# A transformer block on one core: mLSTM cells as two chunks of 128 positions with a carried state, two heads per exponential, product and score bank

## The chip, the cores and the metric

The kernel runs on one core of a Trainium2 chip, as one launch. The metric is the device time in microseconds (us) of that launch, less is better. The engines named below are TensorE (PE; PEld is its weight load), VectorE (DVE), ScalarE (ACT), GpSimd (POOL) and SyncE (SP), which issues most transfers.

## The reference

Four sublayers act on x of 4 x 256 tokens with 256 features: a cross attention, a mixture of 8 expert FFNs (one shared, seven routed), an mLSTM cell, and an FFN with 4-bit block quantisation. The change is in the third one. With queries q from the layer norm of x, keys and values both from `ctx`, 16 heads of 16 features, 256 positions s and t:

```
log_f = log_sigmoid(fg);  log_f_cum = cumsum(log_f)
log_D[s, t] = log_f_cum[s] - log_f_cum[t] + ig[t]   (t <= s, else -inf)
max_log_D = max over t;  D = exp(log_D - max_log_D)
C = (q k^T / sqrt(16)) * D
h = C / (max(|sum_t C|, exp(-max_log_D)) + eps) @ v
h = layer norm over each head's 16 features, times ln_scale
```

## The kernel before

Tokens are worked on in two halves of two batches. The order of all steps is one hand-written list, `step_order` (line 121): each engine walks through the same list and performs its part of the steps that it has. `weave(main, side)` (line 102) spreads the side list over the main one in proportion to TensorE items. Engines are in order, and wait for each other by semaphores.

The cells of half 0 are spread over the experts of half 1 (`expert(k)`, line 159: `gate` and `up` twice, `out` twice, weight splitting, and one step of FFN weight quantisation, `mx_quantise` and `mx_grids`). The cells of half 1 run near the start of the FFN (`stage_d`, line 223), with little beside them.

For each half, `prepare` (line 207) makes the gates: `gate_rows` (a matmul, 32 rows for each batch), `gate_math` on DVE (line 1517: a running sum, a running maximum, and the maximum split into three bf16 parts that six copies place in `mb`), and `q_split`, which cuts the queries into bf16 parts that go through DRAM and come back stacked. `turn_gates` (line 922) waits on TensorE for the end of `gate_math` and for an exponential on ACT, and turns the gate rows into columns `geT`.

Then come 32 cell units w for each half (64 in all), one per head and batch. A unit has the keys as rows, the queries as columns, and only the causal part: 256 columns for keys 0 to 127 and 128 columns for keys 128 to 255.
- `cell_exponent` (lines 933 and 1166): three bf16 matmuls of 256, 256 and 128 columns place the causal mask and minus the running maximum in a bank; ACT takes the exponential in two instructions, each with the key's own gate as a bias column.
- `cell_score` (lines 947 and 1543): two bf16 matmuls of 256 and 128 columns give the scores; DVE multiplies both into `probs` (384 columns).

`cell_bank` (line 87) gives the half 0 units one bank for exponents (4) and one for scores (5); in half 1 there are three of each. So in half 0 the scores of unit w + 1 wait until DVE has done the product of unit w.

Eight units make a group g. `cell_values` (line 959) multiplies them with the values, with f32 matmuls of 32 output rows, four side by side in the array; `cell_values_copy`, `turn3` and `cell_normalise` (line 1554) finish the group. `finish` (line 211) does the head norm and the next layer norm.

## Time and profile before

| | |
|---|---|
| median of 3 runs | 485.39 us |
| the three runs | 485.39, 479.90, 485.39 us |
| the profiled execution | 480.16 us |
| its span, first to last instruction | 478.3 us |
| mean granted TensorE clock | 0.921 of full |
| busy | PE 77%, DVE 75%, ACT 39%, POOL 33% |

The span is what the trace covers; 1.9 us of the profiled execution lie around it. The profiled execution is at the lower of the two levels that the runs show, 5.2 us under the median. Times below count from the span's start.

### The profile page before, as it was taken

Reading aid. Unit: us, or ns where it says so; the run is one execution under the profiler, and the core shown is the slowest. Engines: PE = TensorE matmul, PEld = TensorE weight load, DVE = VectorE, ACT = ScalarE, POOL = GpSimd, SP = SyncE. Lnnn points to the kernel's source line nnn. Section 1 sums busy time; section 2 is a strip of 40 time slices with the busy share of each in tenths; the row PEclk is TensorE's granted clock in tenths of the full one; section 3 lists DMA queues with packets and bytes.
Section 4 is the critical chain, followed back from the end, with each engine's and each line's share of the span. In section 5 each row is a group of like instructions: output and inputs, shape, how many; then the busy total and the mean of one; then the engine's idle time right before and its main releaser. Section 6 shows DMA issues by size and latency. Waiting matters only on the chain.

```text
span 478.3 us, 6936 instructions
## 1 busy us (share of the span) xinstructions
PE 367.9 (77%) x2330; PEld 248.8 (52%) x2330; DVE 359.5 (75%) x857; ACT 188.4 (39%) x331; POOL 155.6 (33%) x147
## 2 busy tenths in 40 slices
PE   7899788999999678957948888977656488650764
PEld 4576456545568457846635565656533156430333
DVE  4588348685549999699796667569995986789895
ACT  4456427233232204412354354533005488540331
POOL 4019400087416325554325413123412110031240
PEclk9999999899999879999979999999888789976687
DMA  8900000032120222234973911824000760000001
GB/s 281 254 28 1 10 1 2 0 112 84 48 67 14 75 89 88 89 88 115 227 123 82 172 56 46 131 57 56 0 1 0 122 122 1 2 0 6 18 19 47
DMA packets 33713, 32.67 MB, mean 68 GB/s; under 512 B 3876, under 2 KB 32784, under 8 KB 33680
## 3 DMA queue, kind: packets, MB, share of 16 engines
q1 hardware_dynamic: 31088, 28.99, 26.1%
q0 software_dynamic: 992, 1.68, 1.1%
q10 hardware_dynamic: 1600, 1.57, 1.0%
q8 instruction: 19, 0.31, 0.3%
q14 instruction: 14, 0.11, 0.1%
HBM read 28.04 MB, written 4.19 MB: 67 GB/s over the span
## 4 chain that ended last, share of the span: by engine, by line
PE 45%; DVE 31%; issue 12%; ACT 8%; POOL 3%; DVEq 0%; ACTq 0%; POOLq 0%
PE bank L870 10%; PE bank L782 5%; PE bank L896 5%; PE bank L755 3%; PE bank L798 3%; PE bank L1006 2%; PE bank L970 2%; DVE mxraw L1624 2%; DVE x L1458 2%; DVE mam L1466 2%; DVE probs L1551 2%; PE bank L766 2%; PE bank L918 2%; PE bank L832 1%; ACT probs L1078 1%
## 5 line engine op out<-in xcount | busy, mean ns | idle before, releaser
L870 PE MATMUL bank<-tok_r,probs_r 128*128 128x512 f32 x104 | 46.6, 448 | 17.4 <-DVE wT L1447 9.7
L896 PE MATMUL bank<-wexp,wT 128*128 128x256 f32 x192 | 53.5, 403 | 6.0 <-DVE x L1458 5.9
L1128 ACT ACTIVATE silu_sb<-bank 128x512 f32<-128x512 f32 x32 | 19.1, 598 | 79.3 <-PE bank L870 79.3
L673 POOL TENSOR_TENSOR wexp_r<-wexp,probs_r 128x1024 fp32r<-128x1024 f32 x13 | 31.3, 2409 | 48.1 <-ACT probs_r L1089 48.1
L1325 DVE TENSOR_SCALAR probs<-probs,hi 128x512 f32<-128x512 f32 x64 | 35.0, 599 | 14.8 <-ACT probs L1078 14.7
L591 POOL TENSOR_TENSOR mx_grid<-parts,bl 128x1024 bf16<-128x1024 fp8e4 x9 | 17.2, 1908 | 88.5 <-DVE parts L1627 88.5
L1078 ACT ACTIVATE probs<-bank 128x1024 f32<-128x1024 f32 x32 | 32.2, 1026 | 29.8 <-PE bank L782 29.8
L896 PEld LDWEIGHTS bank<-wexp,wT 128*128 128x128 f32 x192 | 36.6, 200 | 13.1 <-issue 6.7
L1551 DVE SCALAR_TENSOR_TENSOR probs<-bank,dexp 128x384 f32<-128x384 f32 x48 | 26.5, 555 | 21.2 <-PE bank L956 15.3
L870 PE MATMUL bank<-tok_r,wexp_r 128*128 128x512 f32 x104 | 41.7, 401 | 0.0
L576 POOL TENSOR_TENSOR mxraw<-mxraw,mx_grid 128x512 f32<-128x512 f32 x12 | 15.3, 1278 | 69.6 <-DVE mx_grid L1492 69.6
L782 PE MATMUL bank<-qrep,krep 32*128 32x256 f32 x256 | 33.8, 393 | 2.2 <-ACT probs L1078 1.2
L1175 ACT ACTIVATE dexp<-bank,geT 128x256 f32<-128x256 f32 x48 | 23.2, 483 | 27.9 <-PE bank L944 27.8
L870 PEld LDWEIGHTS bank<-tok_r,probs_r 128*128 128x128 f32 x104 | 20.2, 194 | 24.2 <-DVE wT L1447 11.0
L782 PEld LDWEIGHTS bank<-qrep,krep 32*128 32x128 f32 x256 | 23.1, 184 | 13.7 <-issue 12.3
L955 PE MATMUL bank<-qrep,krep 128*128 128x256 bf16 x64 | 18.0, 281 | 15.5 <-DVE probs L1551 13.6
L996 PE MATMUL bank<-identb,mx_grid 128*128 128x128 bf16 x80 | 8.7, 274 | 27.1 <-POOL mx_grid L591 19.9
L1006 PE MATMUL bank<-ctx,wexp 128*128 128x512 bf16 x64 | 23.0, 519 | 8.0 <-DVE wexp L1636 5.8
L1458 DVE SCALAR_TENSOR_TENSOR x<-bank,cw,x 128x256 f32<-128x256 f32 x64 | 27.5, 475 | 0.1
L1447 DVE SCALAR_TENSOR_TENSOR wT<-silu_sb,bank 128x512 f32<-128x512 f32 x24 | 16.4, 685 | 12.8 <-PE bank L870 5.8
L870 PE MATMUL bank<-xnT_r,probs_r 128*128 128x512 f32 x64 | 25.6, 400 | 0.0
L870 PE MATMUL bank<-xnT,wexp 128*128 128x512 f32 x48 | 24.7, 642 | 0.0
(261 smaller groups left out, 891.1 us busy)
## 6 DMA issues: line engine op xcount, KB each, us to landing
wexp<-in_L_ffn_W SPq DMA_DIRECT2D x28, 256.0 KB, 4.0
krep<-part_dram SPq DMA_DIRECT2D x32, 128.0 KB, 5.3
qrep<-part_dram SPq DMA_DIRECT2D x32, 128.0 KB, 4.8
wexp<-in_L_ffn_Wg SPq DMA_DIRECT2D x14, 256.0 KB, 4.3
part_dram<-parts POOLq DMA_DIRECT2D x4, 384.0 KB, 3.0
part_dram<-parts SPq DMA_DIRECT2D x4, 384.0 KB, 2.6
x<-in_x ACTq DMA_DIRECT2D x2, 512.0 KB, 7.2
ctx<-in_ctx SPq DMA_DIRECT2D x2, 512.0 KB, 6.9
```

Of the source, the lines that this page charges most:

```text
L673: gp.tensor_tensor(low, raw, w_high[k % 2].bitcast(F32), ALU.subtract).then_inc(s["w_low_ready"], 1)
L782: m = pe.matmul(bank[:, bk + q, S * kc:S * kc + S], krows[strip, jj % 2, c, S * b + P * kc:S * b + P * kc + P], qrows[strip, c, S * b:S * ...
L870: mm = pe.matmul(bank[:, bk, :], lhs, rhs, start=(kk == 0 and q == 0), stop=(kk == KC - 1 and q == len(terms) - 1))
L896: mm = pe.matmul(bank[:, 2 + pair, D * t:D * t + D], hid[k % 2][m][:, col:col + P], wexp[:, k % WR, 2, m, :], start=(m == 0), stop=(m == 1))
L955: pe.matmul(bank[:, bk, 0:S], krep[:, slot, j, col:col + P], qrep[:, slot, j, col:col + S], start=True, stop=True)
L1006: m = pe.matmul(bank[:, 2 * (y % 2) + r, :], xqT[:, k, P * i:P * i + P], wt[:, k, 512 * hf:512 * hf + 512], start=(k == 0), stop=(k == KC ...
L1078: act.activation(score_probs(u), bank[:, bk:bk + 2, :], ACT.Exp, scale=1.0 / float(np.sqrt(HD))).then_inc(s["exp_done"], 1)
L1128: act.activation(silu_sb[:, w % 2, :], bank[:, 0, :], ACT.Silu if direct else ACT.Tanh, scale=1.0 if direct else 0.5).then_inc(s["sigmoid_ ...
L1175: act.activation(dexp_slot(w)[:, 0:S], bank[:, bk, 0:S], ACT.Exp, bias=geT[:, n, 0, 0, row:row + 1]).then_inc(s["d_done"], 1)
L1325: ins = v.tensor_scalar(w, w, hi[:, 2 * b + kc:2 * b + kc + 1], EM50, ALU.min, ALU.max)
L1458: v.scalar_tensor_tensor(x[:, i, :], bank[:, 2 + pair, D * t:D * t + D], cw[:, i, e:e + 1], x[:, i, :], ALU.mult, ALU.add).then_inc(s["x2_ ...
L1551: v.scalar_tensor_tensor(probs[:, g % 2, j, 0:384], bank[:, cell_bank(w)[1], 0:384], 1.0 / float(np.sqrt(HD)), dexp_slot(w), ALU.mult, ALU ...
```

## The change

A batch's 256 positions are cut into two chunks of 128. Inside a chunk the cell is computed as before, with a mask, exponents, scores and values of 128 x 128. What the queries of chunk 1 get from the keys of chunk 0 no longer goes through exponents and scores. The keys of chunk 0, weighted by their decay up to position 127, are multiplied with the values into a state of 16 x 17 for each head (`state`), the queries of chunk 1 are weighted by their own decay (`spread`, `qstate`), and two f32 matmuls of 128 x 128 x 128 for each group add state times query into the values' bank.

A unit is now two heads. Its exponents are four blocks of 128 columns that fill a bank (512 columns), its scores four matmuls of 128 columns, with one exponential and one product for both. There are 16 units for each half, four to a group. The key's gate is no bias column of the exponential any more but is added in the matmuls, from a second row that `mb` now carries, so the split into bf16 parts and the six copies are 512 wide.

`gate_math` is cut into `gate_scan`, `gate_split`, `gate_decay` and `gate_place`. `turn_gates` moves from ahead of the cells to behind the first unit, and the cells of half 0 begin behind expert 10's last step instead of within that expert. POOL's share of the quantisation moves from the list's `mx_quantise` to its `mx_grids`, and POOL builds a few more constants.

```
 def cell_bank(w):
-    return (4, 5) if w < 32 else (w % 3, 3 + w % 3)
+    return (4, 5) if w < 16 else (w % 3, 3 + w % 3)
...
-        for j in range(8):
-            w = 8 * g + j
+        for j in range(4):
+            w = 4 * g + j
...
             if g > first:
-                if j == 2:
+                if j == 1:
                     u = st("cell_values", g - 1) + u + st("cell_values_copy", g - 1)
-                if j == 5:
+                if j == 3:
                     u = st("turn3", g - 1) + u + st("cell_normalise", g - 1)
+            if g % 4 == 0:
+                u = [[], st("turn_gates", g // 4), st("spread", g // 4), st("state", g // 2)][j] + u
+            if g % 4 == 1 and j == 2:
+                u = st("state", g // 2 + 1) + u
...
-            + st("gate_rows", n) + st("q_split", 2 * n) + st("gate_math", n) + st("q_split", 2 * n + 1)
+            + st("gate_rows", n) + st("q_split", 2 * n) + st("gate_scan", n) + st("q_split", 2 * n + 1) + st("gate_split", n) \
+            + st("gate_decay", n) + st("gate_place", n)
...
-    plan += expert(8, 5) + weave(expert(9, 6), prepare(0)[:3] + [[]] + prepare(0)[3:5]) + weave(expert(10, 7)[:6], prepare(0)[5:]) + expert(10, 7)[6:8] + st("turn_gates", 0)
-    plan += weave(expert(10, 7)[8:] + flat([expert(k, k - 3) for k in range(11, 14)]), flat([cells(g) for g in range(4)]) + cells_end(3))
+    first = prepare(0)
+    plan += expert(8, 5) + weave(expert(9, 6), first[:3] + [[]] + first[3:5]) + weave(expert(10, 7), first[5:])
+    plan += weave(expert(11, 8) + expert(12, 9) + expert(13, 10), flat([cells(g) for g in range(4)]) + cells_end(3))
...
-    plan += st("q_turn", 0) + ready[:3] + flat(stage_d(0)[:3]) + ready[3:] + flat(stage_d(0)[3:]) + st("turn_gates", 1)
+    plan += st("q_turn", 0) + ready[:3] + flat(stage_d(0)[:3]) + ready[3:] + flat(stage_d(0)[3:])
...
@@ GpSimd, ahead of the copies into vaug @@
+            for b in range(2):
+                seq.add(gp.memset(state_sb(b), 0.0))
...
@@ GpSimd @@
+            def state(b):
+                gp.wait_ge(s["ge_copied"], n + 1)
+                if b >= 1:
+                    gp.wait_ge(s["state_done"], b)
...
+                gp.tensor_tensor(kdecay.rearrange("p (h d) -> p h d", d=HD), keys, decay.unsqueeze(2).broadcast_to([P, H, HD]),
+                                 ALU.mult).then_inc(s["keys_ready"], 1)
...
@@ TensorE @@
+            def spread(n):
+                pe.wait_ge(s["decay_out"], 2 * (n + 1))
+                claim(6, "qstate_ready", n + 1)
+                claim(7, "qstate_ready", n + 1)
+                for c in range(KC):
+                    for b in (2 * n, 2 * n + 1):
+                        m = pe.matmul(bank[:, 6 + b % 2, P * c:P * c + P], head_rows[32 * b:32 * b + 32, c, :], gtmp[32 * b:32 * b + 32, 4, P:2 * P],
+                                      start=True, stop=True)
...
+            def state(b):
+                pe.wait_ge(s["keys_ready"], b + 1)
+                claim(7, "state_ready", b + 1)
+                w = HC * VS
+                for c in range(KC):
+                    m = pe.matmul(bank[:, 7, w * c:w * c + w], kdecay[:, P * c:P * c + P], vaug[:, 2 * b, w * c:w * c + w],
+                                  start=True, stop=True)
...
             def cell_exponent(w):
+                pe.matmul(bank[:, bk, :].rearrange("p (a t) -> p a t", a=4), identb[:, :], tri[:, :].unsqueeze(1).broadcast_to([P, 4, P]),
                           start=True, stop=False, skip_group_check=True)
+                for q in range(2):
+                    pe.matmul(bank[:, bk, S * q:S * q + S], sel[:, 0, h + q:h + q + 1].broadcast_to([96, P]), mb[:, b, 0:S],
+                              start=False, stop=False, skip_group_check=True)
+                for a in range(2):
+                    m = pe.matmul(bank[:, bk, :].rearrange("p (q t) -> p q t", q=2)[:, :, P * a:P * a + P],
+                                  mb[:, b, S + P * a:S + P * a + P], sel[:, 1, h:h + 2].unsqueeze(2).broadcast_to([96, 2, P]),
+                                  start=False, stop=(a == 1), skip_group_check=True)
...
             def cell_score(w):
+                for q in range(2):
+                    for a in range(2):
+                        at = slice(col + P * a, col + P * a + P)
+                        m = pe.matmul(bank[:, bk, S * q + P * a:S * q + P * a + P], krep[:, slot, j + q, at], qrep[:, slot, j + q, at],
+                                      start=True, stop=True)
...
             def cell_values(g):
+                pe.wait_ge(s["qstate_ready"], n + 1)
+                pe.wait_ge(s["state_ready"], b + 1)
...
+                        if kc == 1:
+                            pe.matmul(bank[:, 6, at:at + P], state_sb(b)[:, 2 * c + half, :], qstate[:, c, b % 2, :],
+                                      start=True, stop=False, skip_group_check=True)
...
@@ ScalarE @@
+            def gate_decay(n):
...
+                act.wait_ge(s["decay_in"], n + 1)
+                act.activation(gtmp[r, 4, 0:P], gtmp[r, 1, 0:P], ACT.Exp, scale=-1.0, bias=gtmp[r, 0, P - 1:P]).then_inc(s["decay_out"], 1)
+                act.activation(gtmp[r, 4, P:S], gtmp[r, 0, P:S], ACT.Exp, bias=last_max[r, :]).then_inc(s["decay_out"], 1)
                 act.wait_ge(s["em_in"], n + 1)
+                act.activation(gtmp[r, 5, :], gtmp[r, 2, :], ACT.Exp, scale=-1.0).then_inc(s["em_out"], 1)
...
             def cell_exponent(w):
...
-                act.activation(dexp_slot(w)[:, 0:S], bank[:, bk, 0:S], ACT.Exp,
-                               bias=geT[:, n, 0, 0, row:row + 1]).then_inc(s["d_done"], 1)
-                act.activation(dexp_slot(w)[:, S:384], bank[:, bk, S:384], ACT.Exp,
-                               bias=geT[:, n, 0, 1, row:row + 1]).then_inc(s["d_done"], 1)
+                act.activation(dexp_slot(w), bank[:, bk, :], ACT.Exp).then_inc(s["d_done"], 1)
...
@@ VectorE @@
+            def gate_split(n):
...
+                seq.add(v.tensor_copy(npart[r, 0, :], both))
+                seq.add(v.tensor_tensor(rest, both, npart[r, 0, :], ALU.subtract))
+                seq.add(v.tensor_copy(npart[r, 1, :], rest))
+                seq.add(v.tensor_tensor(npart[r, 2, :], rest, npart[r, 1, :], ALU.subtract))
...
+            def spread(n):
...
+                v.tensor_tensor(qstate, queries, bank[:, 6:8, 0:S].rearrange("p b (c t) -> p c b t", c=KC),
+                                ALU.mult).then_inc(s["qstate_ready"], 1)
+            def state(b):
...
+                blocks = bank[:, 7, 0:H * VS].rearrange("p (r h v) -> p r h v", r=4, v=VS)
...
+                v.tensor_tensor(state_sb(b).rearrange("p r (h v) -> p r h v", v=32)[:, :, :, 0:VS], blocks, own, ALU.mult).then_inc(s["state_ready"], 1)
...
             def cell_score(w):
...
-                v.scalar_tensor_tensor(probs[:, g % 2, j, 0:384], bank[:, cell_bank(w)[1], 0:384], 1.0 / float(np.sqrt(HD)),
-                                       dexp_slot(w), ALU.mult, ALU.mult).then_inc(s["c_done"], 1)
+                v.scalar_tensor_tensor(probs[:, g % 2, j:j + 2, 0:S], pair(bank[:, cell_bank(w)[1], :]), 1.0 / float(np.sqrt(HD)),
+                                       pair(dexp_slot(w)), ALU.mult, ALU.mult).then_inc(s["c_done"], 1)
```

## Rows read from the trace of the kernel before

**Rows 1.** The page: busy us, share of the span, instructions.
```profile
PE 367.9 (77%) x2330; PEld 248.8 (52%) x2330; DVE 359.5 (75%) x857; ACT 188.4 (39%) x331; POOL 155.6 (33%) x147
```
**Rows 2.** Busy time by stretch: stretch, length, engines' busy us, granted clock, DMA share, GB/s.
```profile
249.00:253.00 4.00, 3.79 (x12) 3.03 (x13) 3.71 (x12) 0.67 (x2) 1.16 (x1) 0.50 0.87 97
253.00:321.00 68.00, 54.73 (x435) 38.70 (x434) 43.37 (x98) 33.13 (x81) 23.18 (x18) 1.00 0.43 89
388.00:415.00 27.00, 21.35 (x258) 15.32 (x255) 19.51 (x47) 21.22 (x64) 0.34 (x1) 1.00 0.20 30
```
**Rows 3.** Waits of PE from 253 to 324: total, times, longest us.
```profile
PE bank L955 <- DVE probs L1551: 11.2, 13, 2.8
```
**Rows 4.** Timeline of PE in half 0's cells: start, us, line, operation, tiles, [idle before].
```profile
254.65 0.48 PE L870 MATMUL bank<-tok_r,probs_r 128*128 128x512 f32 x1
...
256.13 0.28 PE L955 MATMUL bank<-qrep,krep 128*128 128x256 bf16 x1
...
261.25 1.95 PE L896 MATMUL bank<-wexp,wT 128*128 128x256 f32 x8
263.03 0.27 PE L955 MATMUL bank<-qrep,krep 128*128 128x256 bf16 x1
...
270.58 0.28 PE L955 MATMUL bank<-qrep,krep 128*128 128x256 bf16 x1 [1.87 <-DVE probs L1551]
...
270.98 0.22 PE L944 MATMUL bank<-mb,sel 96*128 96x128 bf16 x1
271.04 0.39 PE L906 MATMUL bank<-identb,mq 128*128 128x128 bf16 x4
...
273.13 1.51 PE L970 MATMUL bank<-probs,vaug 128*32 128x256 f32 x32
274.57 0.28 PE L955 MATMUL bank<-qrep,krep 128*128 128x256 bf16 x1
...
321.18 0.48 PE L870 MATMUL bank<-tok_r,probs_r 128*128 128x512 f32 x1
```
**Rows 5.** Timeline of PE ahead of half 0's cells.
```profile
247.97 0.69 PE L929 MATMUL bank<-identf,gtmp 64*128 64x64 f32 x4 [5.50 <-ACT gtmp L1160]
...
250.55 1.06 PE L896 MATMUL bank<-wexp,hid_x 128*128 128x256 f32 x2
...
253.11 0.29 PE L941 MATMUL bank<-tri,identb 128*128 128x256 bf16 x1
```
**Rows 6.** Timeline of DVE around half 0's gate rows.
```profile
240.00 0.43 DVE L1502 CAST parts<-mt 128x512 bf16<-128x512 f32 x1
240.46 0.70 DVE L1504 TENSOR_TENSOR parts<-mt,parts 128x512 bf16<-128x512 f32 x1
241.07 0.68 DVE L1466 TENSOR_REDUCE mx_top<-mxraw 128x16 f32<-128x512 f32 x1
...
243.21 2.64 DVE L1522 TENSOR_TENSOR_SCAN gtmp<-gtmp 64x256 f32<-64x256 f32 x1
...
248.92 1.46 DVE L1540 COPY mb<-npart 32x256 bf16<-32x256 bf16 x6
```
**Rows 7.** Groups of one shape: busy us, mean ns of one.
```profile
L1551 DVE SCALAR_TENSOR_TENSOR probs<-bank,dexp 128x384 f32<-128x384 f32 x48 | 26.5, 555 | 21.2 <-PE bank L956 15.3 <-ACT dexp L1177 5.1
L1128 ACT ACTIVATE silu_sb<-bank 128x512 f32<-128x512 f32 x32 | 19.1, 598 | 79.3 <-PE bank L870 79.3
L1441 DVE SCALAR_TENSOR_TENSOR silu_sb<-silu_sb,bank 128x512 f32<-128x512 f32 x16 | 10.9, 679 | 0.1
...
L603 POOL TENSOR_TENSOR x<-x,arows 128x256 f32<-128x256 f32 x4 | 3.2, 818 | 0.0
```
**Rows 8.** Timeline of DVE at both ends of half 1's cells.
```profile
371.82 0.69 DVE L1522 TENSOR_TENSOR_SCAN gtmp<-gtmp 64x256 f32<-64x256 f32 x1 [0.29 <-ACT gtmp L1155]
...
387.69 1.19 DVE L1551 SCALAR_TENSOR_TENSOR probs<-bank,dexp 128x384 f32<-128x384 f32 x2
...
415.32 1.21 DVE L1466 TENSOR_REDUCE mam<-wexp 128x32 f32<-128x1024 f32 x1
```

More of the change, by code:

```diff
@@ L535, in cell_values @@
                 if g in (1, 3):
[L536 removed]
+                    sp.wait_ge(s["qk_done"], 4 * (g + 1))
                     u = (g + 3) // 2
@@ L661, in _ @@
             seq.wait()
+            seq.add(gp.memset(head_cols, 1.0 / float(np.sqrt(HD))))
+            seq.wait()
+            own = head_cols.rearrange("p (c h) -> p c h", c=KC)
+            seq.add(gp.affine_select(out=own, in_=own, compare_op=ALU.is_ge, fill=0.0, base=0,
+                                     pattern=[[0, KC], [-HD, HC]], channel_multiplier=1))
+            seq.wait()
+            seq.add(gp.affine_select(out=own, in_=own, compare_op=ALU.is_ge, fill=0.0, base=HD - 1,
+                                     pattern=[[0, KC], [HD, HC]], channel_multiplier=-1))
+            seq.wait()
             gp.memset(done_word[:, :], 0.0).then_inc(s["consts_made"], 1)
             gp.wait_ge(s["pv_done"], 8)
+            for b in range(2):
+                seq.add(gp.memset(state_sb(b), 0.0))
+            seq.wait()
             for i in range(NT):
@@ L691, in cell_in @@
                                  lsc[:, :].unsqueeze(1).broadcast_to([P, TH, D]), ALU.mult).then_inc(s["h_scaled"], 1)
-            steps = dict(w_split=w_split, x_split=x_split, mx_quantise=mx_quantise, q_split=q_split, cell_in=cell_in, quantise=quantise)
+            steps = dict(w_split=w_split, x_split=x_split, mx_grids=mx_quantise, q_split=q_split, state=state, cell_in=cell_in, quantise=quantise)
             for name, i in plan:
@@ L969, in cell_values @@
                             h0 = (HC * c + j) * VS
[L970 to L973 removed]
+                            m = pe.matmul(bank[32 * q:32 * q + 32, 6, at:at + P], vaug[:, 2 * b + kc, h0:h0 + 32],
+                                          probs[:, g % 2, j, P * kc:P * kc + P], start=(kc == 0), stop=True, skip_group_check=True)
                 m.then_inc(s["pvc_done"], 1)
@@ L1019, in _ @@
                          wo=wo, xt=xt, route=route, gate=gate, up=up, out=out, mx_turn=mx_turn, gate_rows=gate_rows,
-                         turn_gates=turn_gates, cell_exponent=cell_exponent, cell_score=cell_score, cell_values=cell_values,
-                         turn3=turn3, q_turn=q_turn, gate_up=gate_up, down=down)
+                         turn_gates=turn_gates, spread=spread, state=state, cell_exponent=cell_exponent, cell_score=cell_score,
+                         cell_values=cell_values, turn3=turn3, q_turn=q_turn, gate_up=gate_up, down=down)
             for name, i in plan:
@@ L1205, in _ @@
                          bias_turn=bias_turn, cell_values_copy=cell_values_copy, w_split=w_split, x_split=x_split, xt=xt, route=route,
-                         gate=gate, mx_turn=mx_turn, q_high=q_high, gate_rows=gate_rows, gate_math=gate_math,
+                         gate=gate, mx_turn=mx_turn, q_high=q_high, gate_rows=gate_rows, gate_decay=gate_decay,
                          turn_gates=turn_gates, cell_exponent=cell_exponent, cell_in=cell_in, q_turn=q_turn, gate_up=gate_up)
@@ L1645, in _ @@
                          delta_mid=delta_mid, delta_out=delta_out, route=route, route_rank=route_rank, route_weigh=route_weigh, up=up, accumulate=accumulate, mx_quantise=mx_quantise, mx_grids=mx_grids,
-                         q_split=q_split, gate_rows=gate_rows, gate_math=gate_math, cell_score=cell_score,
+                         q_split=q_split, gate_rows=gate_rows, gate_scan=gate_scan, gate_split=gate_split,
+                         gate_place=gate_place, spread=spread, state=state, cell_score=cell_score,
                          cell_normalise=cell_normalise, cell_in=cell_in, cell_mid=cell_mid, cell_out=cell_out,
```

136 lines of the change are left out of this document (74 added, 62 removed).

## The prediction, made before the change was run

> **What bounds the kernel.** I read the page first: PE and DVE are both busy for three quarters of the span and ACT and POOL for little [rows 1], so no engine is the bound of the whole; each stretch has its own. The busy time by stretch then shows the two places where cells run, 253 to 321 (half 0, with experts) and 388 to 415 (half 1, nearly alone) [rows 2]. In neither is an engine full: half 0 has PE at 54.7 and DVE at 43.4 of 68 us.
>
> What the rest of half 0 is, the waits of PE tell: 11.2 us in 13 waits for the cell product on DVE, up to 2.8 us [rows 3]; DVE in turn stands 5.1 us for exponentials, over both halves [rows 7]. The timeline shows two sorts. Where two units follow each other on PE, the second waits about half a microsecond for the product of the first, since there is one score bank. Where DVE has a quantisation and an `up` ahead of the product, PE stands for longer, as at 270.58 [rows 4].
>
> PE's own work there, from start to start in the timeline [rows 4]: a `gate` or `up` 1.48 (254.65 to 256.13), an `out` 1.78 (261.25 to 263.03), a `values` 1.44 (273.13 to 274.57). A unit's 1024 columns at 2.4 GHz are 0.43, and I take 0.44; a `turn3` is about 0.55 and an `mx_turn` 0.22, read off the same timeline. From 253.11 [rows 5] to 321.18, where expert 14 begins [rows 4]: 12 x 1.48 + 6 x 1.78 + 4 x 1.44 + 32 x 0.44 + 4 x 0.55 + 3 x 0.22 = 51.2 of 68.1 us. **So 16.9 us of half 0 are waits**; that is what the change can win there.
>
> Half 1 is different: DVE's cells last 27.6 us (387.69 to 415.32) [rows 8]; 32 products of 0.555 [rows 7] are 17.8 of it and three normalise steps of about 1.24 are 3.7. Of 27 us PE is busy 21.4, DVE 19.5 and ACT 21.2 [rows 2]: three engines are near their limit and trip each other.
>
> **Cells of half 0, after.** Columns of PE: a pair has 512 for scores (before 768) and 1536 for exponents (before 1280), 2048 as before. The values' columns are the same too: per half bank 128 + 128 + 128 (state) for 256 + 128. PE is won nothing in work. It gets more: `spread`, 4 f32 matmuls of 128 columns, `state`, 4 of 136 columns, at 1.78 / 8 x 2 = 0.45 for 256 columns [rows 4], so 0.22 to 0.24 each, together 1.85 with `turn_gates` at 0.5 behind them: +2.3. 11 x 1.48 (the first `gate` now lies ahead) + 10.7 + 6.0 + 16 x 0.88 + 2.2 + 0.7 + 2.3 = 52.3 us.
>
> Whether 128-column matmuls with new weights each run at their columns: the four of L906 take 0.39, one of 128 columns 0.22 by its own row just ahead, so they are 0.057 apart [rows 4], 53 ns by columns. I take that. The Trainium skill (TensorE: Matmul & The Clock Gate, Back-to-back issue gap) gives about 81 ns for 128 columns sustained with weight loads. By that rule the four score matmuls of a unit would cost 0.1 us more and all 32 units 3 us, were PE the bound throughout; the row speaks against it.
>
> The waits: in the new list each unit has at least one 1.48 us item of an expert between it and the next. DVE's loop is 0.68 for a product of 512 columns, as L1441 [rows 7], and some 0.4 of hand-over, ACT's 0.60, as L1128 [rows 7], likewise; both fit under that item, so the short waits go. I walked DVE through the new order: products 16 x 0.72 instead of 32 x 0.60 (-7.7), `spread` 0.7 and two `state` at 0.5 (+1.7), so 37 of some 55 us. The long waits behind quantise and `up` (1.4 + 1.3 us) now find `out` and `values` (3.2 us) between the units and go as well. The keys' product on POOL, near 0.82 to 1.3 by its 128 x 256 addition [rows 7], stands in its queue behind a weight split of 2.4 us; it has about 5 us between `turn_gates` and `state` on PE, so PE may stand there for up to 1 us, once. I keep 2 us of waits and 1 for a half-speed clock at the start; 6 is the upper bound, a third of before.
>
> **The start of half 0.** Before, PE stands 5.5 us at `turn_gates`, and the `out` behind it runs at a granted clock of 0.50, the 1.2 GHz level, 1.06 a pair instead of 0.59 [rows 2, 5]. After, nothing blocks PE there, but `cell_exponent` 0 waits for `gate_place`, and DVE has before that: scan chain from 241.5, 2.6 (4.5 if the scan takes 2.64 as here and not 0.69 as in half 1 [rows 6, 8]); quantise 2.1 (241.07 to 243.21) [rows 6]; grids 1.3 (three passes like the cast); `up` 1.4 (two like L1441 [rows 7]); `gate_split` 2 x (0.46 + 0.73), by the 128 x 512 cast and subtraction [rows 6], 2.4; an accumulate 0.9; six copies of twice the width, between 1.46 [rows 6] and 2.8 (0.46 each, as the cast), 2.0. Sum 12.7 or 14.6: cells begin at 254.2 to 256.1, I take 255.2, 2.1 later than now, with one `gate` done. Expert 14 begins at 255.2 + 52.3 + 3 = 310.5 instead of 321.2: **-10.7**. What follows is a DVE chain that starts from `turn3` in both orders and keeps its length.
>
> **Half 1.** The chain ahead of the cells is DVE's without a gap (`gate_math`, quantise, products of the FFN), so what is added there counts whole: split +0.8, copies +0.5 (up to 1.3), the small negation 0.2: +1.5. `turn_gates` no longer stands between, but hides under DVE's work either way: 0. Then DVE has 16 x 0.72 + 0.7 + 1.0 + 3 x 1.24 = 16.9. PE has 16 x 0.88 + 3 x 1.5 + 3 x 0.55 + 2.3 = 22.5, of which 3.7 (three exponent and two score steps, `turn_gates`, `spread`) fit ahead of the FFN's last product; 18.8 are left, and a product and a normalise end it, 2. 387.7 + 1.5 + 20.8 + 1.0 of waits = 411.0 for 415.3: **-4.3**. PE is the bound there, by 2 us.
>
> **Elsewhere.** POOL's new constants and the two memsets lie where it idles (before line 636 and before the first weight split); at nothing, and 1 to 2 us if that cover were gone. Loads and stacking are the same, with the waits on the same positions. Sum -15.0: 480.2 - 15.0 = 465.2 for an execution at the profiled one's level. The median stands 5.2 above it; what the new runs' level is I can't tell and go half way: **467.5 us**.
>
> **Rivals.** (a) The long waits stay: DVE's order still puts quantise and `up` ahead of a product, and PE meets it. For it: about 9 of the 16.9 us are such waits. Against: the walk above. Half 0 wins the short waits only, 7 of 16.9 less the 2.1 and 2.3: -3; half 1 -4: 473 at the lower level, 475.5 half way. (b) It doesn't bring what it says: PE's work is equal, its adds and DVE's gate work eat the waits, both halves: within 3 us, 482. (c) Slower: the gate part's exponent matmuls move `sel` with a step of zero in the inner dimension, 512 columns of a unit. No row has such an operand (the mask's repeats whole rows). At full speed they are 0.21; at four cycles a column 0.85, 32 x 0.64 = 20 us on PE, which is the bound: 487. It decides from 15 / (32 x 0.21) = 2.2 more cycles per column. The Trainium skill (SBUF — State Buffer, Door 1: The DMA port swizzle) says that accesses which stay in one 16-byte line go at full bandwidth; by it this rival would not happen, and no row here shows it.
>
> **Chances.** Forecast 0.6, (a) 0.2, (b) 0.12, (c) 0.05, more won than forecast (the scan short, no waits left) 0.03. Range 459 to 479: the best case by the lower level is 461 less 2, and 479 takes in (a) at the upper level; it leaves out most of (b) and (c). A difference of 2%, 9.7 us, is about what a measurement of this kernel can tell from none: faster by more 0.72 (forecast, and part of (a)), within 0.22, slower 0.06.
>
> **What the profile would show.** No wait of PE for the product over 1 us between 255 and 310; expert 14 at 310; `turn_gates` without 5.5 us ahead of it, and instead a stand of some 4 us before the first exponent; unit period on PE 0.88 in half 1; ACT's exponential 0.60 once a unit; copies to `mb` near 0.33. I am wrong if score matmuls stand 80 ns apart, if PE waits at `state` for POOL, or if the clock stays at 0.5 beyond the first unit.

## The result, and the profile after

| | before | changed |
|---|---|---|
| median | 484.86 us (20 runs) | 481.60 us (20 runs) |
| ratio, with 95% interval | 1 | 0.9934 [0.9907, 0.9960] |
| the profiled execution, its span | 480.16, 478.3 us | 482.30, 480.6 us |

The change wins 3.3 us (0.7%) where 18 were forecast (485.4 to 467.5); 481.6 us lies outside the range of 459 to 479. The interval lies below 1, so the change is faster, but by less than 2%; to that the prediction gave 0.22, and 0.72 to more. The profiled execution of the changed kernel is at the upper of its own two levels, that of before at the lower of its own, so the traces are compared from one landmark to the next.

The page of the changed kernel (busy us, share of the span, instructions), for [rows 1]:

```profile
PE 379.6 (79%) x2360; PEld 257.9 (54%) x2360; DVE 356.3 (74%) x833; ACT 164.5 (34%) x239; POOL 163.9 (34%) x168
```

ScalarE lost 24 us of work, where it was far from full; TensorE, the bound of both cell stretches, is busy for 12 us more, at a mean clock of 0.89 for 0.92, so a part of the 12 is the same work at a lower clock. The busy time by stretch of the changed kernel (stretch, length, busy us of the engines, granted clock, DMA share, GB/s), for [rows 2]:

```profile
255.40:264.40 9.00, 2.91 (x7) 1.87 (x8) 8.60 (x18) 0.60 (x1) 4.00 (x3) 0.50 0.41 94
264.40:321.00 56.60, 56.06 (x451) 41.74 (x452) 38.25 (x83) 20.52 (x33) 17.71 (x13) 0.96 0.58 104
388.00:402.00 14.00, 14.00 (x124) 9.90 (x123) 6.13 (x10) 5.20 (x10) 1.81 (x3) 0.76 0.30 32
```

Half 0 (264.4 to 321) has become what the prediction said, TensorE busy for 56.1 of 56.6 us. Its waits from 246 to 321, for [rows 3] (total, times, longest):

```profile
PE bank L913 <- DVE silu_sb L1511: 7.2, 1, 7.2
PE bank L1002 <- DVE mb L1617: 4.3, 1, 4.3
PE bank L1046 <- DVE probs L1644: 0.3, 1, 0.3
PE bank L1002 <- ACT dexp L1248: 0.3, 1, 0.3
```

The 13 waits for the cell product are one of 0.3. But ahead of the cells TensorE now waits twice for VectorE, 11.5 us together, where before it waited 5.5 for `turn_gates` [rows 5]. And half 1 (388 to 402) has TensorE full for 14 of 14 us, but at a mean clock of 0.76, with 124 matmuls; before, it was at 1.00 there.

The same landmarks in each kernel, by their starts: the scan that opens a half's gates, the first exponent on TensorE, the last cell product on VectorE, and the end of the span. All in us. The runs are told in the next section.

| kernel | half 0: scan to first exponent | scan to last product | half 1: scan to last product | scan to end | ratio to before |
|---|---|---|---|---|---|
| before | 9.9 | 73.4 | 43.0 | 106.5 | 1 |
| changed | 17.3 | 68.4 | 45.0 | 109.8 | 0.993 |
| a_again | 17.3 | 68.3 | 45.0 | 109.8 | 0.993 [0.990, 0.997] |
| x_bank | 17.3 | 68.6 | 41.1 | 106.0 | 0.988 [0.984, 0.992] |
| x_order | 17.4 | 67.2 | 42.1 | 106.9 | 0.986 [0.981, 0.992] |
| x_fill | 17.3 | 68.5 | 42.1 | 106.6 | 0.988 [0.983, 0.994] |
| x_nostate | 17.3 | 65.0 | 38.7 | 103.3 | 0.970 [0.964, 0.976] |
| x_round | 17.3 | 67.4 | 41.1 | 106.3 | 0.985 [0.978, 0.992] |
| x_bf16 | 17.3 | 66.1 | 41.3 | 106.6 | 0.984 [0.978, 0.990] |
| x_late | 12.0 | 69.0 | 43.6 | 108.3 | 0.991 [0.987, 0.996] |
| x_flow | 12.0 | 69.5 | | | 0.992 [0.987, 0.997] |
| b_turn | 12.0 | 73.2 | 44.5 | 106.7 | 1.002 [0.996, 1.008] |
| x_pool | 14.0 | 64.6 | 45.1 | 109.8 | 0.984 [0.977, 0.992] |
| x_shift | 17.3 | 68.3 | 45.0 | 109.7 | 0.994 [0.990, 0.998] |
| x_best | 12.0 | 68.4 | 40.4 | 104.0 | 0.986 [0.980, 0.991] |
| x_best2 | 12.0 | 66.9 | 39.1 | 103.9 | 0.978 [0.972, 0.985] |
| x_best3 | 17.4 | 65.0 | 39.1 | 103.6 | 0.973 [0.969, 0.978] |
| x_best4 | 14.0 | 63.1 | 38.8 | 104.2 | 0.968 [0.963, 0.974] |

The profiled execution of x_flow was itself a disturbed one, so its half 1 is left out and its half 0 counts for less.

Against before, the changed kernel wins 6.0 us from `gate` 21 (239.37, now 244.86) to expert 14 (321.18 [rows 4], now 320.68), 1.6 of it ahead of the scan, which now stands before a quantise. It loses 3.3 from the scan of half 1 to the end, 2.0 of it up to the last product. The other 1.3 lie behind that: the FFN's next reduction on VectorE starts 1.9 us behind the start of the last product (415.82 to 417.68), before 0.5 (414.86 to 415.32), since the third normalise step now stands between them and before stood ahead of the last two products. It also loses 5.5 ahead of `gate` 21, where the steps of TensorE and VectorE are the same. 3.8 of that arise in one place: busy time from 78 to 98, before and then changed.

```profile
78.00:98.00 20.00, 18.59 (x114) 10.40 (x110) 15.67 (x54) 9.08 (x13) 2.54 (x4) 0.91 0.01 1
```

```profile
78.00:98.00 20.00, 18.68 (x101) 12.19 (x98) 12.76 (x47) 9.27 (x12) 0.00 (x0) 0.66 0.00 1
```

A clock of 0.66 for 0.91 goes with the upper level. The four profiles with 0.91 there reach half 0's scan at 241.7 (x_best2), 241.9 (x_nostate), 243.2 (before) and 245.0 (x_pool), the others, at 0.53 to 0.74 and b_turn with the code of before among them, at 243.8 (x_flow, 0.74) and 245.3 to 248.2.

### The profile page after: what moved, and what is told of

It is laid out like the page before. It is cut to its first block and busy times, and to the rows that moved or that the text cites. A ratio compares the mean times of both kernels' runs of the same rounds, so it can differ in the third digit from the quotient of the medians.

```text
span 480.6 us, 6802 instructions
## 1 busy us (share of the span) xinstructions
PE 379.6 (79%) x2360; PEld 257.9 (54%) x2360; DVE 356.3 (74%) x833; ACT 164.5 (34%) x239; POOL 163.9 (34%) x168
## 5 line engine op out<-in xcount | busy, mean ns | idle before, releaser
L913 PE MATMUL bank<-tok_r,probs_r 128*128 128x512 f32 x104 | 47.5, 457 | 24.6 <-DVE silu_sb L1511 10.2
L603 POOL TENSOR_TENSOR mx_grid<-parts,bl 128x1024 bf16<-128x1024 fp8e4 x9 | 17.2, 1908 | 84.3 <-DVE parts L1720 84.3
L825 PE MATMUL bank<-qrep,krep 32*128 32x256 f32 x256 | 35.6, 409 | 2.1 <-ACT probs L1152 1.1
L825 PEld LDWEIGHTS bank<-qrep,krep 32*128 32x128 f32 x256 | 24.3, 193 | 13.9 <-issue 12.1
L1644 DVE SCALAR_TENSOR_TENSOR probs<-bank,dexp 128x512 f32<-128x512 f32 x24 | 16.5, 688 | 17.5 <-PE bank L1025 17.4
L1517 DVE SCALAR_TENSOR_TENSOR wT<-silu_sb,bank 128x512 f32<-128x512 f32 x24 | 16.4, 684 | 14.6 <-PE bank L913 5.9
L1248 ACT ACTIVATE dexp<-bank 128x512 f32<-128x512 f32 x24 | 14.3, 598 | 35.3 <-PE bank L1009 35.3
L1080 PEld LDWEIGHTS bank<-ctx,wexp 128*128 128x128 bf16 x64 | 7.1, 121 | 30.2 <-issue 14.5
```

The costliest lines, as they stand in the source:

```text
L603: gp.tensor_tensor(b3(q_out[:, k % 2, :]), b3(q8[:, k % 2, :]), blocks(bl[:, k % 2, 3, :]), ALU.mult).then_inc(s["q_ready"], 1)
L825: m = pe.matmul(bank[:, bk + q, S * kc:S * kc + S], krows[strip, jj % 2, c, S * b + P * kc:S * b + P * kc + P], qrows[strip, c, S * b:S * ...
L913: mm = pe.matmul(bank[:, bk, :], lhs, rhs, start=(kk == 0 and q == 0), stop=(kk == KC - 1 and q == len(terms) - 1))
L1080: m = pe.matmul(bank[:, 2 * (y % 2) + r, :], xqT[:, k, P * i:P * i + P], wt[:, k, 512 * hf:512 * hf + 512], start=(k == 0), stop=(k == KC ...
L1517: v.scalar_tensor_tensor(hid[k % 2][m], silu_sb[:, w % 2, :], 2.0 if direct else 1.0, bank[:, 1, :], ALU.mult, ALU.mult).then_inc(s["h_rea ...
L1644: v.scalar_tensor_tensor(probs[:, g % 2, j:j + 2, 0:S], pair(bank[:, cell_bank(w)[1], :]), 1.0 / float(np.sqrt(HD)), pair(dexp_slot(w)), A ...
```

## The experiments

**Half 1: the banks, the clock.** The FFN's last products stand ahead of half 1's cells on VectorE. The changed kernel's `cell_bank(16)` is bank 1, from which the last but one of them reads (exponent 16 starts at 387.24, when that read is over; the last one reads bank 3). TensorE's timeline of the changed kernel, and of x_bank:

```profile
384.60 0.83 PE L1070 MATMUL bank<-identb,mx_grid 128*128 128x128 bf16 x8
387.24 0.39 PE L1002 MATMUL bank<-tri,identb 128*128 128x512 bf16 x1 [1.81 <-DVE wexp L1729]
```

```profile
384.14 0.85 PE L1070 MATMUL bank<-identb,mx_grid 128*128 128x128 bf16 x8
385.04 0.39 PE L1002 MATMUL bank<-tri,identb 128*128 128x512 bf16 x1
...
387.37 0.40 PE L1025 MATMUL bank<-qrep,krep 128*128 128x128 bf16 x4 [0.30 <-DVE wexp L1729]
```

x_bank:

```
-    return (4, 5) if w < 16 else (w % 3, 3 + w % 3)
+    return (4, 5) if w < 16 else ((w + 1) % 3, 3 + (w + 1) % 3)
```

> The changed kernel with one edit: the second half's units take banks ((w+1) mod 3, 3+(w+1) mod 3) instead of (w mod 3, 3 + w mod 3), so that exponent 16 goes to bank 2, as exponent 32 did before the change, and not to bank 1, where the FFN's last product still reads `up`. Theory A (the bank is what kept PE from running ahead, and the stall sends the cells into half clock): exponents 16 and 17 and score 16 start at once behind q_turn, about 2.6 us ahead of the last product; the stretch from the scan of the gates (370.8 in the changed kernel) to the quantise after the cells (417.7) shrinks from 46.9 us by 1.5 to 4 us, 1.5 us if the half clock stays and 4 if it goes. Theory B (half 1 lost its time because the cells themselves are PE-bound at any clock and the start doesn't matter): less than 1 us off the 46.9.

Exponent 16 comes 1.7 us earlier behind its scan and the last product 3.9 us. But x_order, whose half 1 is untouched, has 3.0 of these 3.9. At the same clock of 1.00 as x_order's, the bank itself is worth 0.9.

x_fill adds unread matmuls at two places ahead of the cells, to keep TensorE busy:

```
+    for _ in range(count):
+        pe.matmul(bank[:, 4, :]..., identb, identb repeated 4 times, start=True, stop=True)
```

> The changed kernel with 22 more matmuls whose results nobody reads (bank 4, bf16, 128x512): 16 ahead of gate_up 3 and 6 ahead of exponent 16, where TensorE stands idle before the second half's cells. Theory A (what the second half lost, it lost to the clock that sat at 1.2 GHz until 395.3, behind the idle time of TensorE before the cells): the granted clock of the cells' first 14 us rises from 0.76 to near 1.00 and the cells end 3 to 4 us earlier beside the scan of the gates. Theory B (the clock is not set by that idle time, or the cells' start isn't PE-bound): the clock in 388 to 402 stays under 0.85 and the end moves by less than 1 us, or is later by the filler's own 2 to 5 us.

The clock from 388 to 402 is 1.00 for 0.76 and the last product comes 3.0 us earlier. That looks like theory A, but x_order reaches the same 42.1 with no filler, so the filler isn't shown to be the reason. a_again is the changed kernel, untouched:

> The changed kernel once more, untouched, beside the other runs of this group. It shows how much of the second half's 45.0 us (scan of its gates to its last product) belongs to the kernel and how much to one execution: two runs with the same code there took 42.1 us, and the changed kernel's own profile showed a second spell of half clock inside the cells (388.5 to 395.3). Theory A (that spell is a property of one execution): its stretch is 42 us here. Theory B (it belongs to the kernel): 45 us again.

It repeats the changed profile to 0.1 us, with the spell, the stretch of clock 0.50 from 388.4 to 395.2 inside the cells, at the same place. So the spell isn't chance of one execution, though the mean clocks of the changed kernel's 20 runs, 0.883 to 0.903, say that they don't all have the same spells. x_shift delays half 1 only:

```
-    seq.add(v.tensor_tensor_scan(row(3), row(4), row(5), 0.0, ALU.add, ALU.subtract))
+    for _ in range(1 + 2 * n):
+        seq.add(v.tensor_tensor_scan(row(3), row(4), row(5), 0.0, ALU.add, ALU.subtract))
```

> The changed kernel with the scan of half 1's gates run three times on the same data, so all of half 1 behind it begins some 1.4 us later, and nothing else. Theory A (half 1's second spell of half clock, 388.5 to 395.3 in two profiles of the changed kernel, depends on where its idle stretches fall in the chip's own rhythm, not on the code): the spell goes or changes and the stretch from the last scan to the last product becomes 42 to 43 us (45.0 before the edit), so that a kernel with more work is not slower. Theory B (the spell belongs to what half 1 does): it stays, the stretch is 45 us and the end 1.4 us later.

The stretch from 388 to 402 has the clock 0.76 and 124 matmuls in a_again too. In x_shift and x_fill, and the like 14 us of x_order:

```profile
388.00:402.00 14.00, 13.43 (x131) 9.44 (x132) 7.25 (x12) 6.68 (x12) 3.14 (x3) 0.87 0.28 32
```

```profile
388.00:402.00 14.00, 14.00 (x155) 10.21 (x153) 8.29 (x18) 6.89 (x13) 2.30 (x3) 1.00 0.37 44
```

```profile
387.60:401.60 14.00, 14.00 (x165) 10.02 (x167) 8.62 (x17) 6.08 (x11) 1.24 (x2) 1.00 0.27 30
```

With 1.4 us more of work ahead of them, x_shift's cells end at the same microsecond: the clock beside them is higher and gives it back. Counted from the last scan the stretch is 43.5, above the 42 to 43 of theory A and below B's 45; B's end 1.4 us later didn't come either. So the same cells take 42 or 45 us by the clock beside them. What decides the clock isn't settled. The time at which half 1 begins doesn't by itself: its scan lies at 369.7 in x_order and 371.3 in x_fill, with 42.1, and at 370.8 in the changed kernel, with 45.0; but x_pool (below), whose scan lies at 365.1, takes 45.1 again, with the spell of 0.50 from 17.7 to 24.6 us behind its scan (17.7 to 24.5 in the changed kernel) and, at the same distance, the same clock and count of matmuls:

```profile
382.40:396.40 14.00, 14.00 (x124) 9.90 (x122) 6.13 (x10) 5.23 (x10) 1.76 (x3) 0.76 0.36 39
```

**The state's price.** x_nostate leaves out the state matmuls, and so the off-diagonal term of the output (each narrow matmul then starts its sum afresh):

```
-    if kc == 1:
-        pe.matmul(bank[:, 6, at:at + P], state_sb(b)[:, 2 * c + half, :], qstate[:, c, b % 2, :], start=True, ...)
```

> The changed kernel without the state matmuls of cell_values (16 of them, float32, 128 columns): it leaves the off-diagonal term out of the output. All else, the state's own build included, is kept. It prices the term of the sum that the prediction put at 1.5 us for each values group. Theory A (a values group costs 2.1 us because 32-column weights pay the same with 128 columns as with 256, and the state's matmuls come on top at 0.1 to 0.2 us each): a group falls from 2.1 to about 1.4 us, the cells of half 1 by 4 x 0.5 to 0.7 = 2 to 3 us. Theory B (the group is set by its 16 narrow matmuls and the state's matmuls are hidden): it stays within 0.2 us of 2.1.

A values group of the changed kernel on TensorE, of x_nostate, and (further down) of x_bf16:

```profile
403.85 0.43 PE L1046 MATMUL bank<-probs,vaug 128*32 128x128 f32 x8
404.21 0.49 PE L1041 MATMUL bank<-probs 128*128 128x128 f32 x2
404.63 0.64 PE L1046 MATMUL bank<-probs,vaug 128*32 128x128 f32 x16
405.20 0.49 PE L1041 MATMUL bank<-probs 128*128 128x128 f32 x2
405.62 0.43 PE L1046 MATMUL bank<-probs,vaug 128*32 128x128 f32 x8
405.98 0.40 PE L1025 MATMUL bank<-qrep,krep 128*128 128x128 bf16 x4
406.21 0.38 PE L1002 MATMUL bank<-tri,identb 128*128 128x512 bf16 x1
...
406.65 0.38 PE L1009 MATMUL bank<-sel,mb 96*128 96x256 bf16 x2
406.87 0.33 PE L1025 MATMUL bank<-qrep,krep 128*128 128x128 bf16 x3
```

```profile
276.43 1.08 PE L1043 MATMUL bank<-probs,vaug 128*32 128x128 f32 x32
277.44 0.40 PE L1025 MATMUL bank<-qrep,krep 128*128 128x128 bf16 x4
```

2.13 us from start to start with the state, 1.01 without, 1.44 before [rows 4]; the trace has two records for each of these float32 matmuls. The narrow matmuls did get cheaper with fewer columns, which neither theory had; the two state matmuls, 0.42 each, and what they cost their neighbours put 1.1 us on top. The last product of half 0 comes 3.4 us earlier, that of half 1 3.3 beside x_order at the same clock: 1.1 for each of the three groups that stand ahead of it.

x_round names the bytes of the state and of the scaled queries as rounded float32:

```
-    state_sb = lambda b: probs[:, b % 2, 0:4, S:S + P]
+    state_sb = lambda b: probs_r[:, b % 2, 0:4, S:S + P]     # qstate likewise
```

> The changed kernel with the state and the scaled queries held in rounded float32 (the second name of the same bytes that the FFN's weight parts use), so that the 16 state matmuls of cell_values are rounded float32 ones, like L913's; no instruction is added or removed. The run without the state matmuls showed a values group at 1.08 us for 2.13, so the two float32 matmuls of 128 columns cost 0.52 us each, not the 0.09 that the prediction's count of columns gave them. Theory A (that cost is float32's own passes): each falls to 0.06 to 0.12 us, a group to 1.2 to 1.4 us, half 0 and half 1 by 3 to 4 us each, 5 to 7 in all and some more if the clock follows. Theory B (the cost is that of any 128-row weight load between the narrow ones): a group stays above 1.8 us and the time within 2 us.

Half of each theory: the two matmuls cost 0.25 each for 0.42, but a group is still 1.80, and a half wins 1.0. x_bf16 takes bfloat16 (`.bitcast(BF16)`) and puts both state matmuls between the chunks:

```
 for kc in range(2):
+    if kc == 1:
+        for half in range(2):
+            pe.matmul(state of both halves)
     for half in range(2): ... the narrow ones
```

> The changed kernel with the state and the scaled queries in bfloat16 and a values group in another order: first the 16 narrow pieces of the first chunk, then the two state matmuls, then the narrow ones of the second chunk, so the change of weight shape between 32 and 128 columns comes twice in a group and not four times. Theory A (the state's price is that of float32's passes plus the change of shape): a group goes from 2.13 us (1.80 with rounded float32, 1.08 without the state) to 1.2 to 1.4 us, both halves together lose 6 to 7.5 us. Theory B (the change of shape and the 128-row load cost the same at any type): a group stays at 1.6 to 1.8.

```profile
281.50 0.65 PE L1048 MATMUL bank<-probs,vaug 128*32 128x128 f32 x16
282.07 0.29 PE L1041 MATMUL bank<-probs 128*128 128x128 bf16 x2
282.29 0.64 PE L1048 MATMUL bank<-probs,vaug 128*32 128x128 f32 x16
282.87 0.40 PE L1025 MATMUL bank<-qrep,krep 128*128 128x128 bf16 x4
```

1.37 us, theory A. Two things change in this run, the type and the order; the two state matmuls now take 0.22 together, and 0.14 is left above the 1.01 without them for two changes of weight shape, where x_round has 0.29 for four. Half 0 wins 2.3 us; half 1 is 0.8 below x_order, with TensorE at half clock for its first microseconds. So the two halves don't give the 6 expected.

**The start of half 0.** VectorE in the changed kernel (start, us), and GpSimd beside it:

```profile
248.23 2.72 DVE L1596 TENSOR_TENSOR_SCAN gtmp<-gtmp 64x256 f32<-64x256 f32 x1
...
251.06 1.12 DVE L1599 TENSOR_TENSOR gtmp<-gtmp 64x256 f32<-64x256 f32 x1
252.11 0.67 DVE L1536 TENSOR_REDUCE mx_top<-mxraw 128x16 f32<-128x512 f32 x1
252.81 1.11 DVE L1538 TENSOR_SCALAR mx_top<-mx_top 128x16 uint32<-128x16 uint32 x1
...
258.13 1.65 DVE L1607 TENSOR_TENSOR dexp<-gtmp,pvs 64x512 f32<-64x512 f32 x1
259.81 1.16 DVE L1609 CAST pvs<-dexp 64x512 bf16<-64x512 f32 x1
```

```profile
248.06 2.35 POOL L705 TENSOR_TENSOR wexp_r<-wexp,probs_r 128x1024 fp32r<-128x1024 f32 x1 [8.24 <-ACT probs_r L1163]
250.38 1.53 POOL L713 TENSOR_TENSOR mt<-xnT,parts 128x512 f32<-128x512 f32 x1
251.99 0.67 POOL L715 TENSOR_SCALAR parts<-mt 128x512 bf16<-128x512 f32 x1
252.75 1.15 POOL L717 TENSOR_TENSOR parts<-mt,parts 128x512 bf16<-128x512 f32 x1
...
257.88 1.35 POOL L590 TENSOR_TENSOR mxraw<-mxraw,mx_grid 128x512 f32<-128x512 f32 x1
259.31 1.38 POOL L594 TENSOR_TENSOR mq<-mxraw,mx_sc 128x512 bf16<-128x512 f32 x1
```

x_pool holds GpSimd's work back and leaves VectorE's alone:

```
 gp.wait_ge(s["mx_scaled"], i + 1)
+if i == 7:
+    gp.wait_ge(s["mb_ready"], 6)         # the six copies into mb
 ... and q_split 1 stands behind cell_exponent 2 in the list
```

> The changed kernel with one edit: in the first half GpSimd's quantise of mx tile 7 waits until the last copy into mb is out, and the split of the queries (3.4 us of GpSimd) stands behind exponent 2, so neither lies beside the gates' chain of VectorE. No instruction of VectorE moves. Theory A (VectorE and GpSimd hold each other up at a memory port, which stretched L1599, L1538, L1607 and L1609 by 3.4 us together): these four run at 0.42, 0.18, 0.69 and 0.43 us as where GpSimd is idle, the chain of 17.2 us becomes 13.5 to 14.5 and exponent 0 starts 13.5 to 14.5 us behind the scan for 17.3. Theory B (the stretched durations are the operations' own here, or come from another source): each stays within 0.1 us of what it was and the chain at 17.

Its VectorE:

```profile
249.03 0.41 DVE L1603 TENSOR_TENSOR gtmp<-gtmp 64x256 f32<-64x256 f32 x1
249.36 0.67 DVE L1540 TENSOR_REDUCE mx_top<-mxraw 128x16 f32<-128x512 f32 x1
250.07 0.17 DVE L1542 TENSOR_SCALAR mx_top<-mx_top 128x16 uint32<-128x16 uint32 x1
...
254.45 0.68 DVE L1611 TENSOR_TENSOR dexp<-gtmp,pvs 64x512 f32<-64x512 f32 x1
255.17 0.42 DVE L1613 CAST pvs<-dexp 64x512 bf16<-64x512 f32 x1
```

Theory A on every number: the four fall from 1.12, 1.11, 1.65 and 1.16 us to 0.41, 0.17, 0.68 and 0.42, the first exponent comes at 14.0 for 17.3, and the last product of half 0 at 64.6 for 68.4. This mend alone takes the ratio from 0.993 to 0.984; with four runs of it the two intervals still touch, so the landmarks are the firmer measure. The scan keeps its 2.7, as the weight split stayed beside it.

The Trainium skill (SBUF — State Buffer, Who interferes with whom) says that VectorE and GpSimd share a pair of ports as an exclusive lock; that a VectorE instruction takes it in a two-port mode, or with two SBUF inputs against a GpSimd instruction that reads SBUF; that whoever comes second is then blocked until the first is done; and that on trn2 `tensor_reduce` never contends. The trace agrees: L1536 takes 0.67 with GpSimd at work and 0.67 without. x_late shows the block at its clearest, VectorE and then GpSimd:

```profile
270.37 2.27 DVE L1553 TENSOR_SCALAR mx_sc<-mx_top 128x16 f32<-128x16 f32 x1
```

```profile
270.26 2.34 POOL L709 TENSOR_TENSOR wexp_r<-wexp,probs_r 128x1024 fp32r<-128x1024 f32 x1
```

An instruction of 0.17 us ends at 272.64, GpSimd's at 272.60.

The order was tried three times. x_order: `gate_split`, `gate_decay`, `gate_place` directly behind `gate_scan`.

> The changed kernel with one edit: in the first half gate_split, gate_decay and gate_place stand directly behind gate_scan, ahead of the quantise of the mx tile and the split of the queries, whose POOL parts then don't lie beside the gates' instructions. Theory A (VectorE's gate chain is stretched by POOL's work at its side, and by the quantise work in its middle; the cells can't begin before it): the chain from the start of the scan to the last copy into mb shrinks from 17.2 us to about 10, exponent 0 starts 2 to 6 us earlier, and gate 28 comes 2 to 5 us earlier. Theory B (the FFN's own order sets the start: gate 21, up 21 and their silu must have passed PE and VectorE before the cells whatever the gates do, so the moved quantise comes back in up 21 and in the FFN): the chain is shorter, but gate 28 moves by less than 1.5 us.

Theory B for the start: the chain is 10.5 us, but TensorE then stands 11.8 us for the `silu` of `up` 21, which is now behind it, and the first exponent is where it was. The last product comes 1.1 us earlier. That can be the clock alone: in the first 5 us of the cells, it is 0.54 in the changed kernel (264.4 to 269.4) and 0.88 in x_order (263.7 to 268.7), and 0.34 of 5 us is 1.7 us, an estimate of what that is worth.

x_late: `gate_place` behind `up` 21, `mx_quantise` 7 and `mx_grids` 7 behind exponents 1 and 2.

> The changed kernel with another order around the first half's start: gate_split behind gate_scan, gate_place behind up 21, and the two quantise steps of mx tile 7 behind exponents 1 and 2, where VectorE has room. In the run with the gates' steps in front, the chain was 10.5 us for 17.2 but the cells began no earlier: TensorE stood 11.8 us for up 21's silu, which now lay behind the chain. Theory A (what sets the start is the sum of VectorE's work between the scan and exponent 0, some 17 us, whatever its order): with 3.4 us of quantise taken out, exponent 0 starts 2.5 to 5 us earlier beside the scan (17.3 us behind it in the changed kernel), and the last product of half 0, 68.4 us behind the scan, comes 2 to 5 us earlier. Theory B (the moved quantise comes back between the cells, where VectorE then is late for the next product): the last product comes less than 1 us earlier.

The start came 5.3 us earlier, as theory A has it, and the last product 0.7 later, which is B's side. One reason is the prediction's own worry, TensorE's wait for the keys' product in GpSimd's queue:

```profile
PE bank L995 <- POOL cmp_ L731: 3.4, 1, 3.4
```

The other is the clock: it is 0.50 from 257.4 to 264.2 and from 274.4 to 277.8, 10.2 us of the cells for 4.6 in the changed kernel (264.4 to 269.0). At half speed the 5.6 us more are worth 2.8, an estimate; with the 3.4 that makes 6.2 of the 6.0 us lost.

x_flow moves weight split 12 and `mx_grids` 7 behind `state` 0.

> As the run with the first half's steps reordered, but with weight split 12 and the second part of the quantise of mx tile 7 behind state 0, so that the keys' product (0.62 us) doesn't stand behind 6 us of other work in GpSimd's queue. Theory A (the 5.3 us won at the start were lost to TensorE's wait of 3.4 us for the keys and to a slower stretch of VectorE beside GpSimd's work): that wait is below 0.5 us and the last product of half 0 comes 64 to 66.5 us behind the scan (68.4 in the changed kernel, 69.0 in that run). Theory B (what is won at the start is lost to the clock, whose half-speed spell moves with the idle time before the cells): 67 us or more.

The wait for the keys went; one of 2.5 for the cell product and one of 2.2 for the quantised tile came. The last product at 69.5 is theory B's "67 or more", and the clock was again at about 0.50 for 10.3 us of the cells (255.8 to 259.2, 272.8 to 279.7). How much of the loss is the moved quantise and how much the clock, no run separates. b_turn asks the same of before, with `turn_gates` 0 behind `out` 19 and the cells behind `gate` 22:

> The kernel before with one edit in its order: turn_gates 0 stands behind out 19 and the first cells behind gate 22, so TensorE has the turn, out 18 and 19 and gate 22 ahead of the gates' wait of 5.5 us. Theory A (the changed kernel's gain of 5 to 6 us in half 0 comes from its pairs: half as many hand-overs between TensorE, ScalarE and VectorE): this edit wins no more than 2.5 us of the 73.4 us from the scan to the last product of half 0. Theory B (it comes from the new order of the start, not from the pairs): 4 to 6 us of it.

0.2 us of 73.4, and ten microseconds in 13 waits for the product are still there. So the gain of half 0 isn't the new start's. It is that of pairs and chunks together, which no run separates.

**Together.** x_best has x_round, x_bank and x_late; x_best2 x_bf16, x_bank and x_flow; x_best3 x_bf16, x_bank and x_order; x_best4 x_bf16, x_bank and x_pool.

> The changed kernel with three edits together: the rounded state, the second half's other banks, and the new order around the first half's start. If each saves on its own stretch (state matmuls 6 to 8 us over both halves, start of half 0 some 3, banks and clock in half 1 some 1 to 4), the sum is 10 to 14 us below the changed kernel, near 468 to 471 us. If they overlap (TensorE waits for VectorE's products once its own work is shorter), 5 to 8 us, 473 to 477.

> The three edits that each moved their own stretch, together: the new order around the first half's start, the bfloat16 state with its regrouped matmuls, and banks (w+1) mod 3 in half 1. Start of half 0: 3 to 5 us; state 6 to 7; banks 1. If they add, 10 to 13 us below the changed kernel on the same chip, near 469 to 471. If VectorE's products become the bound once TensorE has less to do, 6 to 8 us below it.

> The changed kernel with the gates' steps of half 0 directly behind the scan, the bfloat16 state with regrouped matmuls, and the banks (w+1) mod 3 in half 1. It differs from the fastest so far only in the start of half 0: the order whose cells began no earlier but whose last product came 1.1 us earlier, instead of the one that began 5.3 us earlier and ended 1.1 us later. Expected by adding: last product of half 0 at 65 us behind the scan (68.4 in the changed kernel, 66.9 in the fastest so far), half 1 at 38 to 39.5; 9 to 11 us below the changed kernel, 470 to 473 us. If the clock's spells decide more than the order, within 2 us of 474.4 either way.

> The changed kernel with GpSimd's quantise and query split taken out from beside the gates' chain (that alone brought the last product of half 0 from 68.4 to 64.6 us behind the scan), the bfloat16 state (another 2.3 there, 3 in half 1) and the banks (w+1) mod 3 in half 1 (1). If they add: last product of half 0 at 62 to 62.5, half 1 at 38 to 39.5, the whole at 466 to 470 us, some 3 us below the fastest so far (471.4). If the clock's half-speed spells give it back, as they did in half 1 when the second gates were moved: 471 to 473.

Medians 477.95, 474.43, 471.42 and 470.06 us. x_best4 is 3.2% below before and 11.5 us below the changed kernel (481.55 in a_again). It has half 0 at 63.1, not the 62 to 62.5 of the sum, and half 1 at 38.8. x_best and x_best2 missed their sums (3.6 and 7.1 us below the changed kernel for 10 to 14 and 10 to 13), both with the start of x_late or x_flow; x_best3 and x_best4 came out within or at the edge of theirs. With the state in bfloat16, x_best2 to x_best4 hold it in fewer bits than the changed kernel.

## Why the prediction was wrong

Forecast -15.0 at the profiled execution's level, -10.7 in half 0 and -4.3 in half 1; the landmarks show -6.0 and +3.3. So 4.7 us are missing in half 0 and 7.6 in half 1. The start of half 0 is the largest step that failed (3.7), then the clock in half 1 (3.0), the price of the state's matmuls (1.9 in half 1, and a part of the 1.0 left in half 0), and the bank (0.9).

- **Half 0's waits: right.** 16.9 us of waits were to fall to 2; the list of waits has 0.6 behind the first exponent. From there to expert 14 it is 56.3 us (264.38 to 320.68) for 55.3. b_turn shows that the new start didn't do it.
- **"The values' columns are the same too": failed.** It counted a float32 matmul of 128 columns and 128 weight columns like a third narrow one. It costs 0.42 us, and a group 2.13 for the 1.44 to 1.5 taken. In half 0, with four groups ahead of expert 14, that is 2.5 of the 4.0 us by which 56.3 is above the sum's 52.3; most of it went into the 3 us kept for waits and clock. In half 1, with three groups ahead of the last product, it is 3 x 0.63 = 1.9 us.
- **The start of half 0: DVE's chain mis-sized, 17.2 us for 12.7 to 14.6.** The sum took durations from where GpSimd is idle, only the scan with its 2.64 [rows 6], and the new list put GpSimd's quantise (moved to `mx_grids`) and query split beside the chain. The cells began at 264.38, which is 258.9 when the 5.5 us ahead of `gate` 21 are taken off, 3.7 later than the 255.2 forecast. x_pool gives 3.3 of them back, and 3.8 at the last product.
- **Half 1: a unit of 0.88 throughout, and the 3.7 us that "fit ahead of the FFN's last product", failed.** The first takes a clock of 2.4 GHz for all cells and was never said as an assumption: a unit is 0.88 in the second part, as forecast, and up to 1.7 in the first, at 1.2 GHz; 3.0 us by x_order and x_fill. The second overlooked the bank's last reader: 0.9 by x_bank. The chain was +1.3 for +1.5. Of the 7.6 us between -4.3 and +3.3, 3.0 + 1.9 + 0.9 = 5.8 have an experiment; 1.8 are open. One of the prediction's own signs of being wrong is there: the clock stayed at 0.50 beyond the first unit, in half 0 until 269.0 and in half 1 from 388.5 to 395.3.
- **Score matmuls 0.057 apart: right** (four in 0.23, from 405.98 to 406.21 in the changed kernel's timeline above), and with them the doubt cast on the 81 ns of the Trainium skill (TensorE: Matmul & The Clock Gate, Back-to-back issue gap). Copies 0.31 each, product 0.69, exponential 0.60: right.
- **Rivals.** (c) fell: L1009, which moves `sel`, takes 0.22 us for its 512 columns (406.65 to 406.87). (a) fell: the long waits are gone. The result is nearest to (b), 482 us with a chance of 0.12, by another way than it said: not that the waits stayed within equal work, but that gain and loss lay in different places.
- **The level.** Half way between two levels was added (465.2 and half of 5.2 are 467.8, not 467.5). 16 of the 20 runs of before and 17 of the changed kernel's stand at their upper level, so the median needed the whole 5.2, and 2.6 us of the miss are this term. The level goes with a clock spell near 80 to 95 us, in code that the change leaves alone.

## What to carry to other kernels

Price a matmul by its type and the shape of its weights before its columns: one float32 matmul of 128 columns with 128 weight columns cost 0.42 us, nearly seven of the narrow ones with 32 (1.01 / 16), and bfloat16 plus a regrouping took most of it back. When a chain on VectorE is to set a start, look at what GpSimd does in the same microseconds, and hold that back before you reorder the chain. A choice of bank is also a choice of whose last read you wait for.

## What was not expected of the hardware

- A VectorE instruction of 128 x 16 elements took 2.27 us instead of 0.17 beside one GpSimd subtraction of 128 x 1024.
- The same cells took 42.1 or 45.0 us at a clock of 1.00 or 0.76 in their first 14 us. The 45.0 came back in a_again and, with all of half 1 some 6 us earlier, in x_pool; 1.4 us more work ahead of them cost nothing (x_shift). What sets the one or the other is open.
- Narrow float32 matmuls (32 weight columns) of 128 columns cost 1.01 / 16 = 0.063 us each, those of 256 and 128 columns mixed 1.44 / 16 = 0.09.
